# A ternary feed-forward stage: rows kept in float32 with the rounding constant until after their transposes

## The reference, cut to what matters

```
act_quant(x):    s = 127 / clip(max|x| over features, 1e-5); clip(round(x*s), -128, 127) / s
weight_quant(w): s = 1 / clip(mean|w|, 1e-5);                clip(round(w*s), -1, 1) / s
bitlinear(x, w): act_quant(x) @ weight_quant(w).T
z = layernorm(x)
h = silu(bitlinear(z, w1)) * bitlinear(z, w3)        # 704 features
x = x + bitlinear(h, w2)
```

## Time and profile before

| | us |
|---|---|
| median of 3 runs | 1058.47 (1058.32 to 1058.51) |
| the profiled execution, its own time | 1058.0 |
| its span, first to last instruction | 1056.3 |
| TensorE busy | 897.9 (85%) |
| VectorE busy | 833.1 (79%) |
| ScalarE busy | 711.4 (67%) |
| GpSimd busy | 550.6 (52%) |
| the stage of the change, in the span | 77 to 176 |

### The profile page before, as it was taken

How to read it: one execution, slowest core, us unless ns; L and a number is a source line. 1 busy time by engine, 2 the same in 40 slices (tenths; PEclk the granted TensorE clock), 3 DMA queues, 4 the chain that set the end, 5 groups by cost and what they waited for, 6 DMA issues and landing times. The chain is left out here.

```text
span 1056.3 us, 21979 instructions
## 1 busy us (share of the span) xinstructions
PE 897.9 (85%) x6914; PEld 786.4 (74%) x6914; DVE 833.1 (79%) x1996; ACT 711.4 (67%) x2342; POOL 550.6 (52%) x783
## 2 busy tenths in 40 slices
PE   3631676359999999999999999999999999995648
PEld 2630443337999999999999999999999999985637
DVE  7988997777889887888988788888777777776370
ACT  3758444757888877888887787777666666662303
POOL 1000000007777867787776777777666666653025
PEclk9965988769999999999999999999999999997559
DMA  9000000111001010001011000000000000002200
GB/s 338 24 1 0 1 0 0 41 53 38 1 2 42 26 56 2 2 2 42 1 41 47 12 16 12 11 12 17 11 12 11 16 12 11 12 1 74 92 21 20
DMA packets 24287, 29.93 MB, mean 28 GB/s; under 512 B 1584, under 2 KB 19824, under 8 KB 23920
## 3 DMA queue, kind: packets, MB, share of 16 engines
q1 hardware_dynamic: 23792, 27.51, 8.0%
q0 software_dynamic: 384, 1.05, 0.3%
HBM read 25.93 MB, written 2.62 MB: 27 GB/s over the span
## 5 line engine op out<-in xcount | busy, mean ns | idle before, releaser
L1439 ACT ACTIVATE a_p<-a_kT_sc_ps,a_nmax 128x64 f32<-128x64 f32 x512 | 153.8, 313 | 57.4 <-DVE a_nmax L1338 53.0
L1305 POOL TENSOR_TENSOR a_cat<-a_tb,a_mb 128x512 fp32r<-128x512 bf16 x128 | 148.1, 1157 | 83.3 <-DVE a_tb L1357 72.4
L1333 DVE TENSOR_REDUCE a_v<-a_sq 128x6 f32<-128x774 f32 x128 | 122.6, 958 | 86.2 <-ACT a_sq L1458 86.1
L1287 POOL TENSOR_TENSOR a_r<-a_v,a_minus_half 128x6 f32<-128x6 f32 x128 | 172.3, 1346 | 21.6 <-DVE a_v L1333 20.3
L1529 PE MATMUL a_pj_ps<-wp,a_cat 128*128 128x256 f32 x1024 | 155.1, 294 | 2.0 <-POOL a_cat L1305 1.9
L1495 PE MATMUL a_qo_ps<-wq,a_xqf 128*128 128x512 f32 x512 | 151.1, 417 | 0.0
L1529 PEld LDWEIGHTS a_pj_ps<-wp,a_cat 128*128 128x128 f32 x1024 | 129.1, 189 | 18.0 <-POOL a_cat L1305 2.7
L1292 POOL TENSOR_TENSOR a_pn<-a_p,a_rsum 128x256 f32<-128x256 f32 x128 | 78.8, 615 | 98.3 <-DVE a_rsum L1396 98.3
L1587 PE MATMUL a_kT_sc_ps<-a_kT,a_qT 128*128 128x64 f32 x1024 | 128.6, 269 | 0.0
L1587 PEld LDWEIGHTS a_kT_sc_ps<-a_kT,a_qT 128*128 128x128 f32 x1024 | 124.4, 192 | 0.3 <-issue 0.3
L1379 DVE TENSOR_TENSOR a_yb<-a_qo_ps,a_ism 128x512 bf16<-128x512 f32 x128 | 88.5, 692 | 32.1 <-PE a_qo_ps L1517 31.9
(11 more groups left out here) (328 smaller groups left out, 2013.4 us busy)
## 6 DMA issues: line engine op xcount, KB each, us to landing
w_work<-in_wprojT SPq DMA_DIRECT2D x4, 1024.0 KB, 7.4
a_ctx<-in_ctxT SPq DMA_DIRECT2D x32, 128.0 KB, 2.2
x_res<-in_x SPq DMA_DIRECT2D x4, 512.0 KB, 5.3
vT<-in_ctxT SPq DMA_DIRECT2D x2, 1024.0 KB, 9.6
w_work<-in_wqT SPq DMA_DIRECT2D x2, 1024.0 KB, 8.2
w_work<-in_wqxT SPq DMA_DIRECT2D x2, 1024.0 KB, 5.1
w_work<-in_wkvxT SPq DMA_DIRECT2D x4, 512.0 KB, 4.6
out_x<-x_res SPq DMA_DIRECT2D x4, 512.0 KB, 4.6
```

The lines of the kernel that those rows point to most:

```text
L1287: nc.gpsimd.tensor_tensor(r6[:], v6[:], minus_half[:], ALU.pow).then_inc(r_ready, 1)
L1305: nc.gpsimd.tensor_tensor(cat[out8.n % 2][:], tb[:], mb[:], ALU.subtract).then_inc(cat_ready, 1)
L1333: nc.vector.tensor_reduce(v6[:], sq[:], AX.X, ALU.add).then_inc(sums_ready, 1)
L1439: nc.scalar.activation(pe_s[:, a * S:(a + 1) * S], sc_ps[:, a * S:(a + 1) * S], ACT.Exp, bias=nmax[:, a:a + 1], accum_out=psum_s[:, a:a + ...
```

## The change

Seven edits to the stage, and one to the helper that serves it:

- VectorE's bf16 copies are gone: `xq`, `hq` and the constant's subtraction on VectorE. The transposes (L942, L950) now read float32 rows that still hold the rounding constant (`hr`, and `zr`), against the float32 identity; `hT_ps` takes two PSUM banks and `xT_ps` one, in float32. ScalarE's three evictions subtract the constant (function Identity with a bias column, in place of Copy).
- Quantising `z` moves from VectorE ahead of the loop (L825) to ScalarE in the loop, one tile per step (`zr = z*qs + ROUND32`).
- Seven of the 16 tiles of `z` are written by ScalarE ahead of its weight work, nine by VectorE.
- `gam` is made by GpSimd, from `small`.
- `hm`, `hr` and `small` have two buffers; the per-tile copy of the scales goes.
- The pieces for the attention stage move from ahead of the loop into ScalarE's steps 0 to 11: two pieces of 128 columns in each, with a quarter of `wp` (512 columns) in steps 1 to 4 and half of `wv` (512 columns) in steps 5 and 6. Only the scaling of the value pieces (L661) stays ahead of the loop.
- The loop with a register counter becomes 19 or 20 steps written out.

```diff
+def first_uppers_act(act, nc, aw, s):
     raw = first_views(aw)
-    for h in range(KC):
...
-        nc.scalar.activation(v, v, ACT.Copy, scale=scale_col(aw, 2, h)).then_inc(aw["scaled"], 1)
-    act.wait_ge(aw["sums_ready"], 1)
-    for i in range(N_HEADS):
+    if s == 0:
+        act.wait_ge(aw["sums_ready"], 1)
+    for i in range(2 * s, min(2 * s + 2, N_HEADS)):
         head = Head(aw, raw, 0, i)
         nc.scalar.activation(head.of(aw["sets"][0][head.part][0][:]), head.w, ACT.Identity, bias=head.sum
                              ).then_inc(aw["upper"], 1)
...
-    for part in "vp":
-        nc.scalar.activation(aw["sets"][0][part][0][:], raw[part], ACT.Copy).then_inc(aw["upper"], 1)
+    if 1 <= s <= 4:
+        rows = slice((s - 1) * PR // 4, s * PR // 4)
+        nc.scalar.activation(aw["sets"][0]["p"][0][:, rows, :], raw["p"][:, rows, :], ACT.Copy).then_inc(aw["upper"], 1)
+    if 5 <= s <= 6:
+        nc.scalar.activation(aw["sets"][0]["v"][0][:, s - 5, :], raw["v"][:, s - 5, :], ACT.Copy
+                             ).then_inc(aw["upper"], 1)
 # GpSimd
+                for n in range(NT):
+                    pool.wait_ge(top_ready, n + 1)
+                    if n >= 4:
+                        pool.wait_ge(x_added, n - 3)
+                    nc.gpsimd.tensor_scalar(gam[n % 4][:], small[n % 2][:, 0:1], ws[:, 2:3], 1.0 / 127.0, ALU.mult,
+                                            ALU.mult).then_inc(gam_ready, 1)
 # VectorE, ahead of the loop
-                for j in range(NT):
+                nc.vector.scalar_tensor_tensor(nmr[:], k["mean"][:], -1.0, k["rstd"][:], ALU.mult, ALU.mult
+                                               ).then_inc(nmr_ready, 1)
+                for j in range(NT - Z_ACT):
...
-                for j in range(NT):
-                    chain.mark(nc.vector.tensor_scalar(z[:, j, :], z[:, j, :], qs[:, j:j + 1], ROUND32,
-                                                       ALU.mult, ALU.add))
 # VectorE, a step
-                        nc.vector.tensor_scalar(xq[u.o % 2][:], z[:, bass.ds(u.n, 1), :]...,
-                                                -ROUND32, None, ALU.add).then_inc(xq_ready, 1)
-                        nc.vector.tensor_copy(cur[u.o][:], tsc[:, bass.ds(u.n, 1), :]...).then_inc(xq_ready, 1)
...
-                        steps(nc.vector.tensor_scalar(hr[:], hm[:], small[:, 2:3], ROUND32, ALU.mult, ALU.add))
                         wait_unit(dve, hT_ready, mid.before(2))
-                        nc.vector.tensor_scalar(hq[mid.o % 2][:], hr[:], -ROUND32, None, ALU.add).then_inc(hq_ready, 1)
-                        dve.wait_ge(hq_ready, mid.count(1, 1))
+                        nc.vector.tensor_scalar(hr[par][:], hm[:], small[par][:, 2:3], ROUND32, ALU.mult, ALU.add
+                                                ).then_inc(hr_ready, 1)
 # ScalarE
+                act.wait_ge(nmr_ready, 1)
+                for j in range(NT - Z_ACT, NT):
+                    nc.scalar.activation(z[:, j, :], x_res[:, j, :], ACT.Identity, scale=k["rstd"][:, j:j + 1],
+                                         bias=nmr[:, j:j + 1]).then_inc(z_ready, 1)
...
+                first_values_act(act, nc, aw)
                 nc.scalar.preload_act_table(ACT.Silu)
+                act.wait_ge(z_ready, NT)
+                act.wait_ge(qs_ready, 1)
+
+                def quantised(u):
+                    wait_unit(act, xT_ready, u.before(2))
+                    nc.scalar.activation(zr[u.n % 2][:], z[:, u.n, :], ACT.Identity, scale=qs[:, u.n:u.n + 1],
+                                         bias=rounding[:, 0:1]).then_inc(zr_ready, 1)
...
-                        nc.scalar.activation(hqT[par][:, 0:full], hT_ps[:, 0:full], ACT.Copy).then_inc(hqT_ready, 1)
+                        nc.scalar.activation(hqT[par][:, 0:full], hT_ps[:, 0:full], ACT.Identity,
+                                             bias=rounding[:, 1:2]).then_inc(hqT_ready, 1)
...
+                    if nxt.live:
+                        quantised(nxt)
+                    if u.live:
+                        first_uppers_act(act, nc, aw, s)
 # TensorE
-                            last = nc.tensor.transpose(hT_ps[0:m, a * P:a * P + P], hq[par][:, a * P:a * P + m],
-                                                       identb[:])
+                            last = nc.tensor.transpose(hT_ps[0:m, a * P:a * P + P], hr[par][:, a * P:a * P + m],
+                                                       ident[:])
```

More of the change, by code:

```diff
@@ L524, in _ @@
                     sums(m)
[L528 to L564, removed]
 def wait_unit(eng, sem, value):
@@ L728, with __init__, count, before @@
 FIRST_HEAD_AT, FIRST_UPPER_AT, FIRST_LOWER_AT = 1, 5, 6
+class Tile:
+    def __init__(self, n, of=NT):
+        self.n, self.live = n, 0 <= n < of
+    def count(self, per=1, more=None):
+        return self.n * per + (per if more is None else more)
+    def before(self, tiles, per=1):
+        return None if self.n < tiles else (self.n - tiles + 1) * per
 def ternary_ffn_stage(k, aw):
@@ L822, in _, with step @@
                 chain.mark(nc.vector.tensor_scalar(tsc[:, :, 1], amax[:], ws[:, 1:2], None, ALU.mult))
-                chain(nc.vector.reciprocal(qs[:], amax[:]))
-                for j in range(NT):
-                    chain.mark(nc.vector.tensor_scalar(z[:, j, :], z[:, j, :], qs[:, j:j + 1], ROUND32,
-                                                       ALU.mult, ALU.add))
+                nc.vector.reciprocal(qs[:], amax[:]).then_inc(qs_ready, 1)
                 chain.settle()
                 steps = Chain(dve, unit_done)
-                def step(i, o):
-                    u, mid, late = (Unit(i, o, WIDTH, ROUNDS, b) for b in (0, 2, 4))
+                def step(s):
+                    mid, late = Tile(s - 2), Tile(s - 4)
                     if mid.live:
-                        steps.at(mid.count(6))
+                        par = mid.n % 2
+                        hm = hms[par]
+                        steps.at(mid.count(3, 0))
+                        wait_unit(dve, hr_ready, mid.before(2))
                         for c in range(2):
@@ L849, in step @@
[L849 to L859, removed]
+                        wait_unit(dve, gam_ready, mid.before(2))
@@ new lines, in step @@
+                        steps(nc.vector.tensor_reduce(small[par][:, 3:4], hm[:], AX.X, ALU.max,
+                                                      apply_absolute_value=True))
+                        nc.vector.tensor_scalar(small[par][:, 0:1], small[par][:, 3:4], tsc[:, mid.n, 1:2], QUANT_EPS,
+                                                ALU.mult, ALU.max).then_inc(top_ready, 1)
+                        dve.wait_ge(top_ready, mid.count())
+                        steps(nc.vector.reciprocal(small[par][:, 1:2], small[par][:, 0:1]))
@@ L860, in step @@
+                        steps.mark(nc.vector.tensor_scalar(small[par][:, 2:3], small[par][:, 1:2], tsc[:, mid.n, 1:2],
+                                                           127.0, ALU.mult, ALU.mult))
                     if late.live:
-                        dve.wait_ge(y_ready, late.count(1, 1))
-                        xt = x_res[:, bass.ds(late.n, 1), :].rearrange("p a c -> p (a c)")
-                        nc.vector.scalar_tensor_tensor(xt, y_ps[:, 0:C], gam[late.o][:], xt, ALU.mult, ALU.add
+                        dve.wait_ge(y_ready, late.count())
@@ L864, in step @@
+                        dve.wait_ge(gam_ready, late.count())
+                        xt = x_res[:, late.n, :]
+                        nc.vector.scalar_tensor_tensor(xt, y_ps[:, 0:C], gam[late.n % 4][:], xt, ALU.mult, ALU.add
                                                        ).then_inc(x_added, 1)
@@ L895, in step @@
                             act.wait_ge(h_ready, mid.count(2, c + 1))
-                            act.wait_ge(xq_ready, mid.count(2, 2))
                             wait_unit(act, hm_ready, mid.before(1, 2))
                             nc.scalar.activation(gate[:, c * HH:(c + 1) * HH], h1_ps[c][:, 0:HH], ACT.Silu,
-                                                 scale=cur[mid.o][:, 0:1]).then_inc(gate_ready, 1)
+                                                 scale=tsc[:, mid.n, 0:1]).then_inc(gate_ready, 1)
@@ L900, in step @@
                     if late.live:
[L901 to L902 removed]
+                        par = late.n % 2
+                        act.wait_ge(hT_ready, late.count())
                         wait_unit(act, y_ready, late.before(2))
                         full = (HC - 1) * P
[L905 to L907 removed]
+                        nc.scalar.activation(hqT[par][:, 0:full], hT_ps[:, 0:full], ACT.Identity,
+                                             bias=rounding[:, 1:2]).then_inc(hqT_ready, 1)
@@ L908, in step @@
+                        nc.scalar.activation(hqT[par][0:TAIL, full:full + P], hT_ps[0:TAIL, full:full + P],
```

(32 more changed lines are left out.)

82 lines of the change are left out of this document (35 added, 47 removed).

## The result

The changed kernel takes 1045.9 us (median of 4, 1044.14 to 1046.17) against 1058.39 (1057.42 to 1058.51): a ratio of 0.9878, 95% interval 0.9866 to 0.9890, 12.5 us less. The forecast was 1045.0, within 1040.5 to 1051.0. The profiled execution took 1044.14 with a span of 1042.4, against 1058.0 and 1056.3.

A forecast was written before the change was run, and what follows sets the result against it. VectorE bounded the loop before; a 3.98 us chain through TensorE would bound it after. The stage would end at 162.1 instead of 176.34, 14.2 us less, taken as 13.5: 1045.0 us, range 1040.5 to 1051.

The forecast's parts named there:

- VectorE ahead of the loop, 91.5; ScalarE, 91.75: Ahead of the loop: VectorE has qs at 91.5, ScalarE finishes the SiLU table at 91.75, the later by 0.3 us.
- First product at 93.5: Start of the loop: the first hidden product starts at about 93.5 instead of 99.41, 5.9 us gained.
- VectorE's step falls to 3.4: In the loop: VectorE's step falls from 4.27 to 3.4 us, so VectorE stops being the bound.
- The chain of 3.98: In the loop: products, transposes, eviction and y through TensorE take 3.98 us a tile and become the bound.
- ScalarE's load shows only in the first steps: In the loop: ScalarE's 3.85 us at most stays under 3.98 and shows only in the first steps, 10.6 us together.
- GpSimd's gam costs nothing: In the loop: gam on GpSimd has two whole steps and costs nothing unless it takes over 6 us.
- The clock: TensorE's clock in the loop: no more half-clock stretches expected, but each half-clock tile would cost 2.4 us more.
- A: Rival, chance 0.20: one or two stretches at 1.2 GHz fall into the loop; time 1048 to 1050.
- B: Rival, chance 0.04: the clock stays at 1.2 GHz, every tile takes 6.4 us; time 1080.
- D: Rival, chance 0.02: Identity is not in the SiLU table, which is loaded twice a tile in the loop; time 1076.
- C: Rival, chance 0.07: VectorE still bounds the loop, at 3.4 us a tile instead of 3.98; time 1038.
- E: Rival, chance 0.07: ScalarE runs late by VectorE's saving and a round trip keeps the loop at 4.4; 1053 to 1058.

The follow-up runs named there:

- e5: Changed kernel with the attention stage's pieces, wp and wv back ahead of the SiLU table's load: 1057.13 us, ratio 0.9988 to the kernel before.
- e6: Changed kernel with all 16 tiles of z written by VectorE, none by ScalarE: 1046.91 us (median of 2).
- e2: Changed kernel with one more VectorE operation per step (128x512 float32, into a tile nobody reads): 1045.2 us (median of 2).
- e8: Changed kernel with y one step later and ScalarE's three evictions subtracting the constant by an immediate: 1038.3 us, ratio 0.9803 to the kernel before.
- e1: Changed kernel with ScalarE's three loop evictions subtracting the constant by an immediate instead of a bias column: 1042.63 us, ratio 0.9848 to the kernel before.
- e4: Changed kernel with y made one step later on TensorE and added one step later on VectorE: 1039.7 us, ratio 0.9817 to the kernel before.
- e11: Changed kernel with y one step later, immediates in the evictions and 30 float32 matmuls on TensorE ahead of the first tile: 1036.33 us, ratio 0.9791.
- e3: Changed kernel with the hidden row back in bf16 and its evictions a plain Copy, z's path as changed: 1046.32 us.
- e9: Changed kernel with the hidden row back in bf16 and y one step later: 1047.5 us (median of 2), ratio 0.9893 to the kernel before.
- e7: Kernel before the change with all 16 steps written out instead of the register-counter loop, nothing else: 1057.4 us, ratio 0.9989.
- e10: Changed kernel with y one step later, immediates in the evictions and one more VectorE operation per step: 1044.09 us (median of 2), ratio 0.9861.

## Why the prediction was right

- **VectorE ahead of the loop, 91.5; ScalarE, 91.75** (its terms as written add to 91.65). 90.93 and 91.25, in a stage that began 0.3 earlier. Seven tiles of z on ScalarE took 3.55, forecast 3.5 between 2.6 and 4.3. That ScalarE is the later by 0.3 was right, and runs show both sides of it: e5 (its load moves the start by all of itself) and e6 (without its help VectorE is late by 2.0).
- **First product at 93.5.** 93.27; 16.32 us into the stage against 22.16: 5.8 gained, forecast 5.9. zr takes 0.60 and not 0.5.
- **VectorE's step falls to 3.4 and is no longer the bound.** Shown by e2, which found the slack, and by e8, where the step is VectorE's own 3.36.
- **The chain of 3.98** (its terms add to 3.99). 4.02. Its terms in the steady step: products 1.21 (forecast 1.20), transposes to eviction 0.85 (0.88), eviction to y 1.10 (1.13), y to the next products 0.86 (0.78). The bias column costs 0.09 an instruction (793 against 703 ns, 350 against 258), taken at 0.10 between 0 and 0.14; e1 took it away and got it back. That this chain bounds is shown by e1 and e4. The only term off by more than 0.03 is y's 0.78: six steps of 0.13 leave out 0.08 between y's last matmul and the next product, which before was hidden in TensorE's wait for hm.
- **ScalarE's load shows only in the first steps.** The fourth product started 10.8 after the first (104.07), forecast 10.6; e5, without the pieces in the loop, took 10.6.
- **GpSimd's gam costs nothing.** 0.26 us each, read two steps later.
- **The clock.** The loop began at half clock, which the walk of its first steps had in it, and was at full clock from 98.1 to the stage's end, as I expected for the likeliest case; before, one half-clock stretch fell into it. The reason that I gave does not stand on good numbers: the trace has TensorE busy 3.10 us of a 4.02 us step after and 2.95 of the 4.53 us step before, not 3.3 and 3.2. The share did rise, but that this kept the clock up is not shown, and no run separates transposes from other matmuls. Rivals A, B and D had no case here: no ACT_TABLE_LOAD between 92 and 162, no slice below 1.00 from 100 to 162. What half clock costs in the last tiles is seen between e8 and e11, 1.4 us; in the steady steps no run shows it. B, the loop at half clock throughout, was in no run.
- **C** (VectorE still the bound, 1038) fell with e2. **E** was wrong in its number, 4.4, but half true in kind: the loop's new bound is a chain of waits through several engines. And undoing one part that has nothing to do with float32 (e5) takes back 9.9 of 13.4.
- **The sum.** 162.1, with 0.7 for small idle times 162.8, which is a stage of 85.55 us from 77.25; measured are 85.71 from 76.95 to 162.66. From the first product to the last it took 59.0 against 58.4 by the terms: 0.2 more in the first steps and 12 times 0.04. The 0.7 was a round allowance, not worked out from rows; that it is so near to this 0.7 is luck. The profiled time is 1044.14 against 1044.5; the median, 1045.9, is 0.9 above my 1045.0, because the spans of the other three executions are 1.4 to 2.0 us longer than the profiled one's. No profile shows where that lies in them; the profiles of the experiments differ by as much ahead of the stage.

What the prediction did not see is which edit earned what. It took float32 rows for the way to a shorter step; the sizes for the other answer were in it (VectorE's step with hq is 3.4 + 0.5 = 3.9, the chain with float32 3.98), and they were not set side by side. e3 and e9 did that. In this kernel the float32 rows cost 0.1 us a tile with the bias column (4.02 against 3.92) and gain 0.08 without it (e1's 3.84); once y is late they gain 0.4 (e4's 3.52) to 0.56 (e8's 3.36).

## What to carry to other kernels

When work leaves the engine that bounds, add up the longest chain that goes through one step of the loop before counting the gain: products, transposes, eviction and next matmuls were 3.56 us against 4.3. The rows of the kernel before show one wait in it, y's 0.75 us for the eviction, but the step was VectorE's. If the new bound is such a chain, look for a result that is made and used in the same step and use it one step later; here that needed no new buffer and brought 6.8 us. And price each edit alone: most of this change's gain hangs on 9.9 us of unrelated ScalarE work that moved from a serial stretch into idle time of the loop. It is worth that much only together with the edits that shortened VectorE's share of the same stretch: before, both engines ended near 98, so moving ScalarE's work alone should have gained little, an argument that no run here tests.

## What the runs showed of the hardware that I had not expected

- The granted clock of TensorE fell to 0.50 in the last tiles of the stage in some profiles (before, e3, e7 to e10) and held through the last matmul in the others (the changed kernel, e1, e2, e4, e5, e6, e11). In e8 it fell at 151.6; in the two stretches of 2 us from 148 on TensorE was busy 1.36 and 1.00, and its longest idle time there was 1.64 us. In e11, with the same code in those tiles and the same idle time of 1.64, the clock held. In the kernel before it fell at 133.2 in the middle of the loop, with no idle time of TensorE over 0.83 us since 107. Why it falls stays open. It cost about 1.4 us between e8 and e11, so differences of that size between two profiles are no proof of an edit.
- A constant as an immediate in a Copy, instead of Identity with a bias column, is 0.09 us shorter on ScalarE, at 640, 256 and 128 columns alike (793 against 704 ns, 463 against 372, 350 against 258).
- Six float32 transposes take 0.82 us at full clock and six bf16 ones 0.61. The weight load of a float32 one takes 140 ns (median in the changed kernel), that of a bf16 one 98 (before).
